# Values products of a first attention in four column groups, and the clearing of a row buffer moved to other stages

## What is computed

```python
x = x + _layernorm(attn(_layernorm(x), Wq, Wk, Wv, Wo))
x = x + _layernorm(ffn(_layernorm(x), ...))
```

```python
sim = jnp.einsum('bhsd,bhtd->bhst', q, k) * scale
weights = softmax(where(causal, sim, -inf))
out = jnp.einsum('bhst,bhtd->bhsd', weights, v)
```

## Time and profile before

| | |
|---|---|
| three runs | 1265.78, 1269.1, 1270.26 us; median 1269.1 |
| the profiled execution | 1271.58 us, of which the span is 1269.8 us |
| TensorE matmul / weight load | busy 94% / 79% of the span |
| VectorE, ScalarE, GpSimd | 68%, 63%, 46% |
| granted TensorE clock, mean | 0.985 |
| DMA | 139.54 MB, mean 110 GB/s |
| `xs_rows` <- `blank` | 31 DMAs of 1040 KB, 1 of 1170 KB |
| `sum_rows` <- `blank` | 3 DMAs of 2176 KB |

### The profile page before, as it was taken

One profiled execution on the slowest core, in us unless ns is written; L12 is line 12 of the kernel. 1 busy time (PEld: TensorE's weight loads), 2 busy tenths in 40 slices (PEclk: granted clock), 3 DMA queues, 4 the chain that ended last, 5 costly groups with the idle time before them and its releaser, 6 DMA issues.

```text
span 1269.8 us, 24366 instructions
## 1 busy us (share of the span) xinstructions
PE 1200.0 (94%) x7612; PEld 1005.0 (79%) x7612; DVE 860.2 (68%) x2630; ACT 793.9 (63%) x1971; POOL 578.1 (46%) x845
## 2 busy tenths in 40 slices
PE   6899998989999999999999999999998889999987
PEld 5745454568989999999998999989997768999962
DVE  5666877737667766787666886677875955555535
ACT  3466777657766777677776777776776534444422
POOL 3052645444334535346542447342463356666650
PEclk9889999989999999999999999999999989999998
DMA  4477777631552011112211112111123236777766
GB/s 150 138 223 231 229 231 223 197 104 64 169 162 67 34 68 34 67 35 101 68 65 37 61 57 91 62 48 53 34 89 99 70 118 119 118 118 118 118 106 221
DMA packets 111682, 139.54 MB, mean 110 GB/s; under 512 B 11269, under 2 KB 94725, under 8 KB 111429
## 3 DMA queue, kind: packets, MB, share of 16 engines
q1 hardware_dynamic: 97108, 119.10, 30.3%
q0 software_dynamic: 14448, 18.88, 9.2%
HBM read 63.36 MB, written 61.87 MB: 99 GB/s over the span
## 4 chain that ended last, share of the span: by engine, by line
PE 67%; DVE 9%; ACT 7%; POOL 6%; DMA 4%; issue 4%; SPq 3%; POOLq 0%; ACTq 0%; DVEq 0%
PE bank L1441 45%; PE bank L1523 5%; PE bank L1827 4%; PE bank L1645 4%; PE bank L1490 3%; DMA raw_qkv<-in_qkvo 2%; DVE bank L1086 2%; POOL sum_rows L721 2%; ACT p L926 1%; PE bank L1510 1%; ACT pT L811 1%; PE bank L1517 1%; POOL xs_rows L659 1%; DVE hs L1299 1%; POOL w_hl L513 1%
## 5 line engine op out<-in xcount | busy, mean ns | idle before, releaser
L1086 DVE CUSTOM_DVE_ANT_0 bank<-bank,mask 128x512 f32<-128x512 f32 (+3 forms) x512 | 235.6, 522 | 49.5 <-PE bank L1510 36.3
L917 ACT ACTIVATE p<-bank,stat 128x512 f32<-128x512 f32 (+3 forms) x256 | 131.5, 526 | 132.3 <-DVE stat L1086 132.3
L512 POOL CAST w_hl<-raw_qkv 128x512 fp32r<-128x512 f32 x96 | 58.7, 611 | 316.0 <-DMA raw_qkv<-in_qkvo 173.1
L1441 PE MATMUL bank<-xT,w_hl 128*128 128x512 f32 x768 | 189.4, 395 | 2.4 <-POOL w_hl L513 2.4
L1441 PEld LDWEIGHTS bank<-xT,w_hl 128*128 128x128 f32 x768 | 144.1, 188 | 36.7 <-POOL w_hl L513 2.8
L721 POOL DMA_INDIRECT sum_rows<-mid,goal x79 | 122.8, 1555 | 70.9 <-DVE mid L1405 68.9
L1441 PE MATMUL bank<-pT,v 128*128 128x128 f32 (+3 forms) x768 | 137.1, 327 | 0.0
L926 ACT ACTIVATE p<-p,stat 128x512 f32<-128x512 f32 (+3 forms) x256 | 123.1, 553 | 14.7 <-DVE stat L1302 14.7
L1441 PE MATMUL bank<-qk 128*128 128x512 f32 (+3 forms) x768 | 129.4, 317 | 2.6 <-DVE pT L1286 2.6
L1441 PEld LDWEIGHTS bank<-qk 128*128 128x128 f32 x768 | 119.2, 189 | 11.3 <-DVE v L1280 2.8
L513 POOL TENSOR_TENSOR w_hl<-raw_qkv,w_hl 128x512 fp32r<-128x512 f32 x96 | 124.1, 1293 | 7.8
(11 more groups left out here) (232 smaller groups left out, 2455.4 us busy)
## 6 DMA issues: line engine op xcount, KB each, us to landing
xs_rows<-blank SPq DMA_DIRECT2D x31, 1040.0 KB, 5.0
raw_qkv<-in_qkvo SPq DMA_DIRECT2D x32, 768.0 KB, 5.3
xrow<-xs_rows SPq DMA_DIRECT2D x79, 130.0 KB, 2.5
raw_o<-in_qkvo SPq DMA_DIRECT2D x32, 256.0 KB, 3.3
sum_rows<-blank SPq DMA_DIRECT2D x3, 2176.0 KB, 9.8
stk<-xT SPq DMA_DIRECT2D x96, 64.0 KB
stk<-k_hl SPq DMA_DIRECT2D x96, 64.0 KB
yl<-sum_rows SPq DMA_DIRECT2D x24, 256.0 KB, 6.2
```

The lines of the kernel that those rows point to most:

```text
L512: link(pool.tensor_copy(hi, raw))
L917: act.activation(p2[:, n % 2, POFF[qi]:POFF[qi + 1]], s2(t), ACT.Exp, scale=-1.0, bias=stat2[:, 0, n % 2, t:t + 1], accum_out=stat2[:, 1, ...
L1086: return dve.tensor_tensor_reduce(scores, scores, mask[:, TB - scores.shape[1]:], scale=-1.0, scalar=-2.0 * MASKED, op0=ALU.add, op1=ALU.m ...
L1441: ins = pe.matmul(out, a, b, start=start and i == 0, stop=stop and i == len(pairs) - 1, **kw)
```

## The change

It does four things.

1. In the first attention a values product is cut by queries as well. Head a and half v take column group 2a + v. Half 0 has the query blocks 0 and 3, half 1 the blocks 1 and 2. Each step now uses all four groups, and the two steps that share bank 6 lie beside each other in its columns. A step has 14 values products in place of 8: four of 256 columns for n = 4, then two of 128 and two of 256 for n = 3, four of 128 for n = 2, and two of 128 for n = 1.
2. `weigh` divides each half by itself: two reciprocals and two multiplies in place of one each. The turn of `o` picks its blocks in the new order (`Q_SLOT`).
3. The three `sum_rows` and the first 40 tiles of `xs_rows` are cleared in the prologue, ahead of the first stack. Each step of the first attention then clears 2 tiles.
4. The last 153 tiles are cleared in the second attention, at j = 1 to 5, in pieces of 30, 31, 30, 31 and 31 tiles, each where the clearing of a `sum_rows` stood.

```diff
+        Q_GROUPS = ((0, 3), (1, 2))
+        Q_SLOT = (0, 1, 3, 2)
...
+        CLEAR_FIRST, CLEAR_STEP, CLEAR_LATE = 40, 2, 5
...
-            def prefill(s):
-
-                xs = xs_d.rearrange("(n p) c -> p n c", p=P)
-                each = E * CAP // P // N1
-                some = slice(each * s, each * (s + 1) + (1 if s == N1 - 1 else 0))
-                sp.dma_start(xs[:, some, :], blank[:, :].unsqueeze(1).to_broadcast([P, some.stop - some.start, ROW]))\
+            def clear(rows_d, width, some):
+
+                sp.dma_start(rows_d.rearrange("(n p) c -> p n c", p=P)[:, some, :],
+                             blank[:, 0:width].unsqueeze(1).to_broadcast([P, some.stop - some.start, width]))\
                   .then_inc(d_zero, 16)
 
             sp.wait_ge(d_blank, 2)
+            for a in range(NSUM):
+                clear(sum_d[a], D, slice(0, T + 1))
+            clear(xs_d, ROW, slice(0, CLEAR_FIRST))
             sp.wait_ge(stk_zero, 3)
             sp.wait_ge(ph1_lo, 4)
...
-                prefill(s)
+                first = CLEAR_FIRST + CLEAR_STEP * s
+                clear(xs_d, ROW, slice(first, first + CLEAR_STEP))
...
-                if j <= NSUM:
-                    sp.dma_start(sum_d[j - 1].rearrange("(n p) d -> p n d", p=P),
-                                 blank[:, 0:D].unsqueeze(1).to_broadcast([P, T + 1, D])).then_inc(d_zero, 16)
+                if j <= CLEAR_LATE:
+                    first = CLEAR_FIRST + CLEAR_STEP * N1
+                    left = E * CAP // P + 1 - first
+                    clear(xs_d, ROW, slice(first + left * (j - 1) // CLEAR_LATE, first + left * j // CLEAR_LATE))
...
-                    heads = free[:, :].rearrange("p (j h n) -> p j h n", j=TPB, h=4)
-                    link(dve.reciprocal(o1_rec[:, :, :].unsqueeze(3), heads[:, :, :, DH1:DH1 + 1]))
...
+                    link(*[dve.reciprocal(rec[:, :, v, :].unsqueeze(3), heads[:, :, v, :, DH1:DH1 + 1])
+                           for v in range(2)])
...
+                    for v in range(2):
+                        ins = dve.tensor_tensor(own[:, :, v, :, :], heads[:, :, v, :, 0:DH1],
+                                                rec[:, :, v, :].unsqueeze(3).to_broadcast([P, 2, 4, DH1]), ALU.mult)
...
-                def value(r, a, n):
-
-                    kj, j = TPB - n, 2 * (r % 2) + a
-                    return pe.matmul(bank[O1_BANK][2 * DH1 * j:2 * DH1 * (j + 1), P * kj:TB], v1_pad[:, r % 2, kj, a, :],
-                                     pt1(r, a, n), start=n == TPB, stop=n == 1, skip_group_check=True)
+                def values(r, n):
+
+                    kj = TPB - n
+                    for a in range(2):
+                        for v in range(2):
+                            queries = [q for q in Q_GROUPS[v] if q >= kj]
+                            if queries:
+                                ins = pe.matmul(o1_part(r, a, v, queries), v1_pad[:, r % 2, kj, a, :],
+                                                pt1(r, a, n, queries), start=kj == 0, stop=kj == max(Q_GROUPS[v]),
+                                                skip_group_check=True)
+                    return ins
```

More of the change, by code:

```diff
@@ L279, in st1, with pt1, o1_part @@
             return bank[3 + (5 * s + i) % 3]
-        def pt1(s, a, n):
+        def pt1(s, a, n, queries):
             i, first = item(a, n)
-            return pT1[:, s % 2, i, first:first + P * n]
+            at = [first // P + q - (TPB - n) for q in queries]
+            return pT1[:, s % 2, i, :].rearrange("p (c n) -> p c n", n=P)[:, at[0]:at[-1] + 1:max(1, at[-1] - at[0]), :]
+        def o1_part(s, a, v, queries):
+            own = bank[O1_BANK][2 * DH1 * (2 * a + v):2 * DH1 * (2 * a + v + 1), :]
+            at = [Q_GROUPS[v].index(q) for q in queries]
+            return own.rearrange("p (i r n) -> p i r n", i=2, r=2)[:, at[0]:at[-1] + 1, s % 2, :]
         def s2(t):
@@ L610, in constants @@
                 whole = hot[:, :, :, :].rearrange("p t k e -> p (t k e)").bitcast(I32)
-                pool.wait_ge(d_zero, 16 * (N1 + NSUM))
+                pool.wait_ge(d_zero, 16 * (NSUM + 1 + N1 + CLEAR_LATE))
                 pool.wait_ge(m_y, 2 * B)
@@ L1139, in weigh @@
                     dve.wait_ge(a1_ot, i + 1)
-                    heads = free[:, :].rearrange("p (j h n) -> p j h n", j=TPB, h=4)
-                    link(dve.reciprocal(o1_rec[:, :, :].unsqueeze(3), heads[:, :, :, DH1:DH1 + 1]))
[L1142 to L1145, removed]
+                    heads = free[:, :].rearrange("p (i h v n) -> p i v h n", i=2, h=4, v=2)
+                    rec = o1_rec[:, :, :].rearrange("p (i v) h -> p i v h", i=2)
+                    link(*[dve.reciprocal(rec[:, :, v, :].unsqueeze(3), heads[:, :, v, :, DH1:DH1 + 1])
+                           for v in range(2)])
+                    own = o1[:, :, 4 * DH1 * (i % 4):4 * DH1 * (i % 4 + 1)]\
+                        .rearrange("p (i v) (h n) -> p i v h n", i=2, h=4)
+                    for v in range(2):
+                        ins = dve.tensor_tensor(own[:, :, v, :, :], heads[:, :, v, :, 0:DH1],
+                                                rec[:, :, v, :].unsqueeze(3).to_broadcast([P, 2, 4, DH1]), ALU.mult)
+                    ins.then_inc(a1_xo, 1)
                 if s + 1 < N1:
@@ L1543, in step1 @@
                     pe.wait_ge(a1_sel, 4 * (s - 1) + 1)
-                    for a in range(2):
-                        value(s - 1, a, TPB)
+                    values(s - 1, TPB)
                 if s >= 3 and s % 2 == 1:
@@ L1582, in step1 @@
                     for n in range(TPB - 1, 0, -1):
-                        for a in range(2):
-                            ins = value(s - 1, a, n)
+                        ins = values(s - 1, n)
                     ins.then_inc(a1_pv, 1)
@@ L1588, in step1 @@
                     pe.wait_ge(a1_xo, 2 * g + 2)
-                    turn(lambda j: o1[:, j, P * (g % 2):P * (g % 2 + 1)], a1_xt, free)
+                    turn(lambda j: o1[:, Q_SLOT[j], P * (g % 2):P * (g % 2 + 1)], a1_xt, free)
                 if b >= 0 and k == 2:
```

## The result

| | before | changed |
|---|---|---|
| median of the runs compared | 1268.58 us (4 runs, 1265.78 to 1270.26) | 1283.7 us (4 runs, 1282.74 to 1288.96) |
| span of the profiled execution | 1269.8 us | 1281.0 us |
| mean granted clock | 0.985 | 0.973 |

The ratio is 1.013, with a 95% interval of 1.0096 to 1.0163: slower, by 15 us in the medians and by 11.2 us in the two profiled spans. The forecast was 1280.7 us for the median and 1283.2 us for the profiled execution, which took 1282.7.

The account below looks back on a forecast made before the run. The prediction took a loop between TensorE and ScalarE as the bound, with SP close to the pace. -20 + 27.6 + 4 = +11.6 us on 1271.6 gave 1283.2 profiled, 1280.7 for the median; range 1262 to 1299.

Parts of the forecast that it names:

- Speed of four column groups: First attention, TensorE: values products for n = 4 fall from 0.98 to 0.56 us, for n = 3 to 1 from 1.42 to 0.83.
- the first rival: First attention: four groups don't run side by side, or instruction issue is the bound; 1293 to 1301 us; chance 0.13.
- First attention, -20 us: First attention: shorter values products and no waits for stacks gain 20 us in all, between -5 and +34.
- the loop of TensorE and ScalarE: First attention: the two engines wait for each other, neither is the bound; values products for n = 3 to 1 lie on it.
- The third rival: First attention: SP was the pace more than counted, its freedom gives 28 us and not 20; 1266 us; chance 0.15.
- Prologue, nothing: Prologue: clearings put ahead of the stacks cost nothing; first stack lands near 50 us, first scores stand at 55.27, cover 5 us.
- C: Second attention: time of a clearing piece of 31 tiles, 4.13 MB; taken as 12.5 us, between 12.0 and 13.1.
- The second rival: Second attention: loads don't wait for the whole clearing, a piece acts as 6 us; 1256 us; chance 0.12.
- The chain, +27.6 us: Second attention, pairs 2 to 5: late `raw_qkv` delays GpSimd's splits, these `raw_o`, and the next piece; 27.6 us lost.
- Clock, +4 us: Second attention: stalls at pairs 4 to 6 drop the granted clock to half; 4 us added, between 0 and 9.

## Why the prediction was right

The kernel is slower, by the steps that were forecast, and 1283.7 us is 3.0 over the number given. The parts are not as close as the sum.

- **Speed of four column groups.** 0.56 and 0.83 us were forecast, 0.57 and 0.79 measured: the groups run side by side, and the first rival falls. Twenty instructions in 0.79 us are 40 ns each. The Trainium skill, "TensorE: Matmul & The Clock Gate", section "Part 1", would want 62 ns each with hardware decoding off, 1.24 us; here that isn't borne out, and no view shows which way of decoding this run used.
- **First attention, -20 us.** -17.1 at the end of the stage and -18.6 from turn to turn. Of the 1.5 us between these two, 1.1 are that the first turn stands later (61.77 against 60.69), as the first scores do. The six other kernels with the same prologue have their first scores at 54.24 to 55.26 us, so the clearing isn't its cause. It is the scatter of single executions: two of these kernels have the changed kernel's instructions up to `raw_qkv` of pair 1 and issue it at 245.48 and 246.87 us, which makes the gain 20.2 and 18.8. The two steps at half clock cost 1.5 us each, which the sum had no term for; without them it would be 20 us here. That neither part would bring it alone was not in the argument. I counted the loop of TensorE and ScalarE, and 2.5 us for SP. The clearing alone is worth 2.1 us in this stage, much as counted. But the values products alone are worth 1.6 and not 17: the sum of the parts was right for the two together and would have been wrong for one.
- **SP as the pace.** The third rival gave SP's freedom 28 us. With 2 tiles a step it gives 2 alone, and the stage's gain stays at 17: that rival falls too. What it had right is that SP was close, closer than my 2.5 us of waits for stacks say: it was hardly ever idle in the old loop, and left as it was it takes back nearly the whole gain of the values products.
- **Prologue, nothing.** Held: the stack's DMAs were issued until 48.9 us, close to the 50 forecast.
- **A piece of the clearing, C = 12.5 us.** This is the term that was mis-sized. Three places have 13.5 to 14.0, more than the 13.1 that I had as the upper bound, and pair 4 has 12.1. While a piece moved, from 330 to 338 us, the two stretches show 337 and 336 GB/s:

```profile
330.00:334.00 4.00, 4.00 (x23) 3.47 (x22) 2.05 (x9) 3.75 (x13) 0.00 (x0) 1.00 1.09 337
334.00:338.00 4.00, 4.00 (x34) 3.87 (x33) 3.02 (x6) 3.21 (x9) 0.00 (x0) 1.00 1.10 336
```

  4.13 MB at that rate are 12.3 us, and the 30 tiles of pair 3 are 11.9. So the rate was right and 1.2 to 2.1 us come on top where the piece stands between two loads. A part of them is that its end is slower: 261 GB/s from 338 to 340 us. No run here separates the rest. At pair 4, where other loads stand behind the piece, nothing comes on top. The Trainium skill, "DMA: Bandwidth & Descriptors", section "Specifications", with 358 GB/s gave an estimate of 11.5 for C; the measured 13.5 to 14.0 decide.
- **The loads wait for the whole clearing.** The second rival had C act as 6 us. More than the whole transfer is seen in three places, and taking the piece at pair 4 away gave back 12.2 us in the trace and 13.6 in the medians. It falls.
- **The chain, +27.6 us.** From `raw_o` of pair 2 (294.75) to the heads of pairs 4, 5 and 6 it is 52.7, then 39.5 and 26.7 us. Forecast were 50.3, 39.9 and 25.6. In all the chain loses 30.7 us against the old kernel, 3.1 more than forecast, and all of that is C (three times 1.0 to 1.5 more, once 0.4 less). TensorE was to stand 7, 18 and 4 us at pairs 4 to 6; it stands 4.9, 16.8 and 3.3, and 2.9 at pair 3, where I had foreseen none. At its start `raw_o` of pair 2 came 0.8 us earlier than the first attention's gain explains: 29.9 us for the stage.
- **Clock, +4 us.** This term should have been zero where I put it. The clock did fall after the stalls, and the products behind them took 4.40 and 5.07 us for 2.95. But each of these is followed by another wait for weights, which GpSimd and the loads set. TensorE's slower work there only shortens its next stall: the stalls of pairs 3 to 6 add up to 27.9 us, 25.5 more than before, where the chain loses 30.7. And the chain doesn't see the clock: from the first split behind `raw_o` of pairs 2, 3 and 4 to `raw_o` of the next pair it is 12.55, 7.75 and 7.74 us, with TensorE at half clock in a part of each, and was 12.65, 7.81 and 7.74 before. Counting the clock beside a chain that it isn't on counted it twice. What the clock did cost, 3 us, lay in the first attention, where I had not looked for it.
- **What was not foreseen** is 1.6 us less behind pair 6. It is scatter. Up to the first load of the sums at the end (`yl`, 1245.3 us, 1231.8 before) the changed kernel is 13.5 us behind. From there to the first store of the output it takes 18.9 us and the old one 21.3, and in the other kernels, whose instructions there are the same, it is anything from 18.7 to 22.7.

So the way is right, and that the total is this close is luck: C, which cost 3 us more than forecast, the clock's 4 us that weren't there, the 3 us less of gain, and 2.4 us that the `raw_o` of pair 2 and the last stage gave, nearly cancel.

## What to carry to other kernels

Two limits of a loop that lie as close together as here (6.1 to 6.3 us and 6.2 us a step) hide each other's price: relieve both in one kernel and each alone before either is called worthless or valuable. Work that must go somewhere, like these clearings, belongs where its queue has slack per step; here four tiles fit into each step for nothing, while the same bytes between a load and the load that the next stage waits for cost their full transfer, once for each time they stand there. And where a chain of transfers sets the time, a slower clock on the engine that waits for it is not added. An effect that moves by itself between executions of the same instructions can't be judged by one trace of each kernel.

## What the runs showed of the hardware that was not expected

- The granted clock fell to 1.2 GHz at 152 and at 200 us, though from 72 to 236 us TensorE waits for no longer than 1.1 us at a time. In the 2 us ahead of the fall at 152 us TensorE was busy 1.26 us. The old kernel stood at the full clock behind a stretch with less work than that. The stretch of the changed kernel, and the one of the old:

```profile
150.00:152.00 2.00, 1.26 (x5) 0.55 (x3) 2.00 (x11) 2.00 (x6) 0.47 (x2) 1.00 0.57 178
```

```profile
146.00:148.00 2.00, 0.75 (x6) 0.44 (x7) 2.00 (x11) 1.39 (x4) 1.74 (x2) 1.00 0.33 91
```

  So the work just ahead doesn't decide it alone. The Trainium skill, "TensorE: Matmul & The Clock Gate", section "Part 1", says that the clock follows how busy TensorE has lately been. These runs don't settle it: the two rows speak against the last 2 us alone, the falls move between executions of the same instructions, and they come only in the kernels with the shorter values products. In all, the first attention of the changed kernel paid 3 us of its gain back in clock.
- What is cleared ahead on SP's queue holds SP at its next issue. The stack's three DMAs behind 12 MB of clearing took 18.70 us to issue. In the second attention the issue of `raw_qkv` takes 0.43 us with nothing ahead of it, 2.0 and 2.3 behind 14 tiles, 4.7 behind 20, 6.2 to 6.4 behind 24, and 8.5 to 9.8 behind 30 to 32.
- The clearing of `sum_rows`, with rows of 1024 bytes, moves faster than that of `xs_rows`, with rows of 1040. Two stretches of the changed kernel's prologue, one in each:

```profile
16.00:20.00 4.00, 4.00 (x12) 3.10 (x12) 0.89 (x7) 0.60 (x1) 0.00 (x0) 1.00 1.08 386
36.00:40.00 4.00, 4.00 (x25) 3.51 (x24) 2.79 (x11) 1.86 (x5) 0.00 (x0) 1.00 1.09 335
```

  No run separates the length of a row from what else differs between the two.
- Four weight loads and matmuls in four column groups start 6 to 7 ns apart (the four from 102.97 us on), and the twenty instructions of 128 columns in 0.79 us come to 40 ns apiece. The earlier trace rows had only two groups at once.
